# A Perceiver layer on one core: another order of work in the opening, and GpSimd's second K piece and first queries given to ScalarE and VectorE

## What is computed

```python
q = (Q @ Wq + bq) / sqrt(64)   # Q = layernorm(x), 16 heads of 64
k = K @ Wk + bk                # K = V = ctx
v = V @ Wv + bv
x = x + (softmax(q k^T) v) @ Wo + bo           # cross attention
x = x + self_attention(layernorm(x))           # latent K/V, decay, 16 heads of 16
x = x + fp4_ffn(layernorm(x))                  # 256 -> 704 -> 256
```

## Time and profile before

| | us |
|---|---|
| three runs, median | 1313.55 |
| lowest, highest | 1306.68, 1316.39 |
| the profiled execution, its own time | 1306.82 |
| its span in the profile | 1305.0 |

### The profile page before, as it was taken

One profiled execution on the slowest core, in us unless ns is written; L12 is line 12 of the kernel. 1 busy time (PEld: TensorE's weight loads), 2 busy tenths in 40 slices (PEclk: granted clock), 3 DMA queues, 4 the chain that ended last, 5 costly groups with the idle time before them and its releaser, 6 DMA issues.

```text
span 1305.0 us, 25086 instructions
## 1 busy us (share of the span) xinstructions
PE 1267.7 (97%) x9210; PEld 1103.3 (85%) x9210; DVE 879.0 (67%) x1405; ACT 882.2 (68%) x1735; POOL 962.3 (74%) x1132
## 2 busy tenths in 40 slices
PE   5899999999999999999999999999999999999898
PEld 5788888888888888888888888888888888777775
DVE  3566667666766677667766676667666776676657
ACT  3677766777677766777667766777676767676752
POOL 4887898679877986788777987798779868537510
PEclk9999999999999999999999999999999999998999
DMA  4010000000000001101000000000000000300000
GB/s 136 18 29 25 17 1 10 9 18 1 2 18 9 25 18 41 35 23 34 9 10 18 1 2 17 17 2 1 18 1 1 2 9 1 106 2 1 1 1 17
DMA packets 24904, 22.97 MB, mean 18 GB/s; under 512 B 4432, under 2 KB 24528, under 8 KB 24784
## 3 DMA queue, kind: packets, MB, share of 16 engines
q1 hardware_dynamic: 24784, 21.38, 5.5%
HBM read 20.85 MB, written 0.52 MB: 16 GB/s over the span
## 4 chain that ended last, share of the span: by engine, by line
PE 85%; POOL 7%; DVE 3%; ACT 2%; issue 2%; DMA 0%; POOLq 0%; ACTq 0%; DVEq 0%
PE psT L681 17%; PE psS L671 14%; PE psW L709 13%; PE psW L722 12%; PE psO L697 9%; PE psO L698 9%; POOL kT L510 2%; PE saO L931 1%; PE saS L904 1%; PE psW L761 1%; POOL kT L509 1%; PE saO L1035 1%; PE psW L731 1%; POOL v L522 1%; PE psW L744 1%
## 5 line engine op out<-in xcount | busy, mean ns | idle before, releaser
L1217 ACT ACTIVATE pT_hi<-psT 128x512 fp32r<-128x512 f32 x512 | 293.3, 602 | 238.1 <-PE psT L681 235.2
L1453 DVE TENSOR_TENSOR pT_lo<-psT,pT_hi 128x512 fp32r<-128x512 f32 x512 | 330.0, 685 | 103.9 <-ACT pT_hi L1217 102.9
L1447 DVE TENSOR_REDUCE negm<-psS 128x1 f32<-128x1024 f32 x256 | 311.6, 1218 | 20.3 <-PE psS L671 16.8
L510 POOL TENSOR_TENSOR kT<-kraw,khi 64x512 fp32r<-64x512 f32 x252 | 324.1, 1286 | 0.0
L1180 ACT ACTIVATE prob<-psS,negm 128x1024 f32<-128x1024 f32 x256 | 285.8, 1116 | 1.0 <-DVE negm L1447 1.0
L681 PEld LDWEIGHTS psT<-ident,prob 128*128 128x128 f32 x2048 | 230.2, 141 | 62.6 <-issue 36.3
L681 PE MATMUL psT<-ident,prob 128*128 128x128 f32 x2048 | 273.4, 276 | 1.5 <-DVE pT_lo L1453 1.4
L697 PE MATMUL psO<-pT_hi,v 128*128 128x256 f32 x1024 | 268.3, 294 | 0.9 <-POOL v L522 0.9
L698 PE MATMUL psO<-pT_lo,v 128*128 128x256 f32 x1024 | 256.8, 282 | 0.0
L1520 DVE TENSOR_TENSOR oT<-psO,olow 64x256 f32<-64x256 f32 x128 | 53.5, 418 | 214.9 <-ACT olow L1389 214.9
L671 PE MATMUL psS<-kT,q_hi 64*128 64x512 f32 x1024 | 194.5, 416 | 3.4 <-ACT prob L1180 2.0
(11 more groups left out here) (281 smaller groups left out, 1673.8 us busy)
## 6 DMA issues: line engine op xcount, KB each, us to landing
cst<-in_ctx_dram SPq DMA_DIRECT2D x12, 512.0 KB, 3.8
wraw<-in_L_xattn_Wk_dram SPq DMA_DIRECT2D x8, 256.0 KB, 2.6
wraw<-in_L_xattn_Wv_dram SPq DMA_DIRECT2D x8, 256.0 KB, 2.6
wraw<-in_L_xattn_Wq_dram SPq DMA_DIRECT2D x8, 256.0 KB, 2.7
wo<-in_L_xattn_Wo_dram SPq DMA_DIRECT2D x8, 256.0 KB, 2.7
oT<-in_ctx_dram SPq DMA_DIRECT2D x2, 512.0 KB, 5.5
prob<-in_ctx_dram SPq DMA_DIRECT2D x2, 512.0 KB, 4.8
ff_wdn<-in_L_ffn_w_down_dram SPq DMA_DIRECT2D x1, 704.0 KB, 7.4
```

The lines of the kernel that those rows point to most:

```text
L510: pool.tensor_tensor(kT[half, m // 2 % KRING, h, 1, :], raw[own, :], khi[own, :].bitcast(F32), ALU.subtract).then_inc(k_split, 1)
L1217: act.activation(pT_hi[:, i % PRING, :], psT[:, t % 2, :], ACT.Copy).then_inc(ph_ok, 1)
L1447: dve.tensor_reduce(negm[:, g % 2, h, qt, c:c + 1], psS[:, qt, :], AX.X, ALU.max, negate=True)\
L1453: dve.tensor_tensor(pT_lo[:, i % PRING, :], psT[:, t % 2, :], pT_hi[:, i % PRING, :].bitcast(F32), ALU.subtract).then_inc(pl_ok, 1)
```

## The change

It reorders the opening on all five queues and moves two splits off GpSimd.

- SP loads Wk right after x, and Wq into the tile of Wo (`wq_first`), ahead of Wv; Wo's first load waits for Wq's split. Context piece 2 is staged in a tile of the later feed-forward part instead of `prob`.
- TensorE turns context units 0 to 3 before xn, then projects k0, k1, q0, v0, q1, v1, k2, runs scores(0), projects v2, k3, v3 and turns units 4 to 7.
- Piece 1 of K is split from PSUM: three activations on ScalarE (`second_piece_high`), two `scalar_tensor_tensor` on VectorE (`second_piece_low`), which add the bias and subtract the high part. Query pair 0 likewise (`first_pair_high`, `first_pair_low`), three and three. `kraw_ok`, `k_split`, `qraw_ok` and `q_ok` count one less from then on.
- GpSimd splits Wk, Wq, Wv, piece 0, query pair 1, pieces 2 and 3.
- The maxima and exponentials of head 0 come before v2, k3 and v3 on VectorE and ScalarE.

The diff, cut to its changed lines (inner indentation shortened):

```diff
@@ before, line 174 @@
-        staging = [oT[:, i, 0:KPP, :] if i < 2 else prob[:, i - 1, :].rearrange("p (k d) -> p k d", k=KPP)
-                   for i in range(FIRST)]
+        staging = [oT[:, i, 0:KPP, :] for i in range(2)] + [
+  tail.win[:, 0, 0:KPP, :], prob[:, 2, :].rearrange("p (k d) -> p k d", k=KPP)]
@@ before, line 192 @@
+        second_h, second_l, pair0_h, pair0_l = (sem(i) for i in ("second_h", "second_l", "pair0_h", "pair0_l"))
+        wq_first_in = sem("wq_first_in")
@@ before, line 230 @@
+        def pieces_split(m):
+  return 4 * (m if m >= 1 else m + 1)
+        def pairs_split(g, p):
+  return 6 * (2 * g + p)
@@ before, line 238 @@
+        khi_second = pT_hi[:, 0, :]
+        wq_first = wo[:, :, :]
@@ before, line 381 @@
-      wait(sp, wk_ok, 2 * max(g, 1))
-      if g == 1:
-          wait(sp, wq_ok, 2)
+      wait(sp, wk_ok, 2 * g)
@@ before, line 392 @@
+      if g == 0:
+          wait(sp, wq_ok, 2)
@@ before, line 403 @@
+  load_k(0)
...
-  load_k(0)
+  sp.dma_start(wq_first, rows(Wq, 0)).then_inc(wq_first_in, 16)
...
-  load_q(0)
@@ before, line 471 @@
-      wait(pool, raw, 16 * (g + 1))
-      src = wraw[:, slot, :, :]
+      if raw is not raw_q:
+          wait(pool, raw, 16 * (g + 1))
+      elif g:
+          wait(pool, raw_q, 16 * g)
+      else:
+          wait(pool, wq_first_in, 16)
+      src = wraw[:, slot, :, :] if g or w_s is not wq_s else wq_first
@@ before, line 481 @@
-      n = 6 * (2 * g + p)
-      wait(pool, qraw_ok, 2 * g + p + 1)
+      n = pairs_split(g, p) - 6
+      wait(pool, qraw_ok, 2 * g + p)
@@ before, line 499 @@
-      wait(pool, kraw_ok, m + 1)
+      wait(pool, kraw_ok, m if m else 1)
...
-      wait(pool, khi_ok, m + 1)
+      wait(pool, khi_ok, m if m else 1)
...
-      wait(pool, k_split, 4 * m + 4)
+      wait(pool, k_split, pieces_split(m))
@@ before, line 549 @@
+  split_w(0, 1, wq_s, raw_q, wq_ok)
...
-  split_piece(1)
-  split_w(0, 1, wq_s, raw_q, wq_ok)
-  for p in range(2):
-      split_q(0, p)
+  split_q(0, 1)
@@ before, line 660 @@
-          wait(pe, k_split, 4 * (n + 2))
+          wait(pe, k_split, pieces_split(n + 1))
+      if n == 0:
+          wait(pe, second_h, 3)
+          wait(pe, second_l, 2)
+          wait(pe, pair0_h, 3)
+          wait(pe, pair0_l, 3)
...
-          wait(pe, q_ok, 6 * (2 * g + h // 2 + 1))
+          wait(pe, q_ok, pairs_split(g, h // 2))
@@ before, line 763 @@
+  for u in range(4):
+      if u % KT == 0:
+          pe.wait_ge(staged[u // KT], 16)
+      turn_ctx(u, staging[u // KT], bank_S[u])
...
-          last = pe.transpose(bank_S[kt][:, r * P:(r + 1) * P], xn[:, r, kt * P:(kt + 1) * P], ident[:, :])
+          last = pe.transpose(bank_T[kt][:, r * P:(r + 1) * P], xn[:, r, kt * P:(kt + 1) * P], ident[:, :])
...
-  for u in range(4):
+  pe.wait_ge(prep_l, 2)
+  project_k(0, psO[:, :])
+  pe.wait_ge(prep_l, 4)
+  project_k(1, psW[:, :])
+  pe.wait_ge(xnT_l, KT)
+  project_q(0, 0, bank_S[0][:, 0:S])
+  project_v(0, bank_S[2])
+  project_q(0, 1, bank_S[1][:, 0:S])
+  project_v(1, bank_S[3])
+  pe.wait_ge(kraw_ok, 1)
+  project_k(2, psO[:, :])
+  pe.wait_ge(qraw_ok, 1)
+  pe.wait_ge(v_lo, 2)
+  scores(0)
+  project_v(2, bank_T[0])
+  project_k(3, psW[:, :])
+  project_v(3, bank_T[1])
+  for u in range(4, 8):
...
-      turn_ctx(u, staging[u // KT], (bank_S[2], bank_S[3], bank_T[0], bank_T[1])[u])
-  pe.wait_ge(prep_l, 2)
-  project_k(0, psO[:, :])
-  project_v(0, psW[:, :])
-  pe.wait_ge(prep_l, 4)
-  pe.wait_ge(xnT_l, KT)
-  project_k(1, bank_S[0])
-  project_v(1, bank_S[1])
-  pe.wait_ge(staged[2], 16)
-  for u in range(4, 6):
-      turn_ctx(u, staging[2], bank_T[u % 2])
-  project_k(2, bank_S[2])
-  project_v(2, bank_S[3])
-  pe.wait_ge(kraw_ok, 1)
-  project_q(0, 0, psO[:, 0:S])
-  pe.wait_ge(v_lo, 1)
-  project_q(0, 1, psW[:, 0:S])
-  pe.wait_ge(kraw_ok, 2)
-  project_k(3, bank_S[0])
-  pe.wait_ge(v_lo, 2)
-  project_v(3, bank_S[1])
-  pe.wait_ge(staged[3], 16)
-  for u in range(6, 8):
-      pe.wait_ge(prep_l, u - 1)
-      turn_ctx(u, staging[3], bank_T[u % 2])
-  pe.wait_ge(kraw_ok, 4)
-  pe.wait_ge(v_lo, 4)
-  scores(0)
-  pe.wait_ge(prep_l, 8)
+      if u < 6:
+          pe.wait_ge(v_lo, u - 1)
+      else:
+          pe.wait_ge(kraw_ok, u - 4)
+      turn_ctx(u, staging[u // KT], (bank_T[0], bank_T[1], psO[:, :], psW[:, :])[u - 4])
...
-          pe.wait_ge(qraw_ok, 2)
+          pe.wait_ge(prep_l, 8)
@@ before, line 1071 @@
-              wait(pe, qraw_ok, 2 * (g + 1) + (k - 13) // 2 + 1)
+              wait(pe, qraw_ok, 2 * (g + 1) + (k - 13) // 2)
@@ before, line 1087 @@
-          wait(pe, kraw_ok, n + LEAD + 1)
+          wait(pe, kraw_ok, n + LEAD)
@@ before, line 1184 @@
-          wait(act, k_split, 4 * (m - 1))
+          wait(act, k_split, pieces_split(m - 2))
@@ before, line 1197 @@
-      wait(act, q_ok, 6 * (2 * (g - 1) + p + 1))
+      wait(act, q_ok, pairs_split(g - 1, p))
...
+  def second_piece_high():
+      wait(act, k_ps, 2)
+      act.activation(khi_second, psW[:, :], ACT.Identity, bias=bkT[:, 0:1]).then_inc(second_h, 1)
+      for h in range(2):
+          own = slice(HD * h, HD * h + HD)
+          act.activation(kT[HD:2 * HD, 0, h, 0, :], psW[own, :], ACT.Identity, bias=bkT[own, 0:1])\
+              .then_inc(second_h, 1)
+  def first_pair_high():
+      wait(act, q_ps, 1)
+      act.activation(q_hi[:, 0, 0, :], bank_S[0][:, 0:S], ACT.Identity, bias=bqT[:, 0:1]).then_inc(pair0_h, 1)
+      for half in range(2):
+          own, other = slice(HD * half, HD * half + HD), slice(HD - HD * half, 2 * HD - HD * half)
+          act.activation(q_hi[other, 1, 0, :], bank_S[0][own, 0:S], ACT.Identity, bias=bqT[own, 0:1])\
+              .then_inc(pair0_h, 1)
@@ before, line 1317 @@
+  for u in range(4):
+      prep_high(u, bank_S[u])
...
-      act.activation(xnT_hi[:, kt, :], bank_S[kt], ACT.Copy).then_inc(xnT_h, 1)
-  for u in range(4):
-      prep_high(u, (bank_S[2], bank_S[3], bank_T[0], bank_T[1])[u])
+      act.activation(xnT_hi[:, kt, :], bank_T[kt], ACT.Copy).then_inc(xnT_h, 1)
...
-  v_high(0, psW[:, :])
-  k_raw(1, bank_S[0])
-  v_high(1, bank_S[1])
-  for u in range(4, 6):
-      prep_high(u, bank_T[u % 2])
-  k_raw(2, bank_S[2])
-  v_high(2, bank_S[3])
-  for p in range(2):
-      q_raw(0, p, (psO, psW)[p][:, 0:S])
-  v_high(3, bank_S[1])
-  for u in range(6, 8):
-      prep_high(u, bank_T[u % 2])
-  k_raw(3, bank_S[0])
+  second_piece_high()
+  first_pair_high()
+  v_high(0, bank_S[2])
+  q_raw(0, 1, bank_S[1][:, 0:S])
+  v_high(1, bank_S[3])
+  k_raw(2, psO[:, :])
...
+  v_high(2, bank_T[0])
+  k_raw(3, psW[:, :])
+  v_high(3, bank_T[1])
+  for u in range(4, 8):
+      prep_high(u, (bank_T[0], bank_T[1], psO[:, :], psW[:, :])[u - 4])
@@ before, line 1458 @@
+  def second_piece_low():
+      for h in range(2):
+          own = slice(HD * h, HD * h + HD)
+          wait(dve, second_h, 3)
+          dve.scalar_tensor_tensor(kT[HD:2 * HD, 0, h, 1, :], psW[own, :], bkT[own, 0:1],
+                                   khi_second[own, :].bitcast(F32), ALU.add, ALU.subtract).then_inc(second_l, 1)
+  def first_pair_low():
+      wait(dve, pair0_h, 3)
+      dve.scalar_tensor_tensor(q_lo[:, 0, 0, :], bank_S[0][:, 0:S], bqT[:, 0:1], q_hi[:, 0, 0, :].bitcast(F32),
+                               ALU.add, ALU.subtract).then_inc(pair0_l, 1)
+      for half in range(2):
+          own, other = slice(HD * half, HD * half + HD), slice(HD - HD * half, 2 * HD - HD * half)
+          dve.scalar_tensor_tensor(q_lo[other, 1, 0, :], bank_S[0][own, 0:S], bqT[own, 0:1],
+                                   q_hi[own, 0, 0, :].bitcast(F32), ALU.add, ALU.subtract).then_inc(pair0_l, 1)
@@ before, line 1700 @@
+  for u in range(4):
+      prep_low(u, bank_S[u])
...
-      dve.tensor_tensor(xnT_lo[:, kt, :], bank_S[kt], xnT_hi[:, kt, :].bitcast(F32), ALU.subtract)\
+      dve.tensor_tensor(xnT_lo[:, kt, :], bank_T[kt], xnT_hi[:, kt, :].bitcast(F32), ALU.subtract)\
...
-  for u in range(4):
-      prep_low(u, (bank_S[2], bank_S[3], bank_T[0], bank_T[1])[u])
...
-  v_low(0, psW[:, :])
-  v_low(1, bank_S[1])
-  for u in range(4, 6):
-      prep_low(u, bank_T[u % 2])
-  v_low(2, bank_S[3])
-  v_low(3, bank_S[1])
-  for u in range(6, 8):
-      prep_low(u, bank_T[u % 2])
+  dve.wait_ge(bq8_ok, 1)
+  second_piece_low()
+  first_pair_low()
+  v_low(0, bank_S[2])
+  v_low(1, bank_S[3])
...
+  v_low(2, bank_T[0])
+  v_low(3, bank_T[1])
+  for u in range(4, 8):
+      prep_low(u, (bank_T[0], bank_T[1], psO[:, :], psW[:, :])[u - 4])
```

## The result

| | before | after |
|---|---|---|
| median of 17 runs each | 1310.52 us | 1297.65 us |
| lowest, highest | 1306.56, 1319.58 | 1295.35, 1305.89 |
| the profiled execution, own time | 1306.82 | 1300.94 |
| its span | 1305.0 | 1299.0 |

The ratio is 0.9912, with an interval from 0.9895 to 0.9929: faster by 0.88%, which is inside the 1% that the prediction took as the limit of what can be told. The prediction was a ratio of 0.9906 (12.4 of 1313.55 us). Two numbers need care. The medians stand 12.9 us apart, the two profiled executions 5.9, and both differ from the 11.5 that the ratio gives on 1306.8.

A forecast was written before the change was run, and what follows sets the result against it. TensorE's matmul queue bounds the body, which follows the opening. Head 0's turn 11.2 us earlier plus 1.48, together 12.6, less 0.2 for handovers: 12.4 off 1313.55, forecast 1301 us (0.94% less), range 1293 to 1309.

The forecast's parts named there:

- Loads: Opening: context lands at 7.0 and 8.5 us, Wk at 5.6, Wq at 9.3; weight splits finish before use.
- The 0.3 us that the prediction put beside the sum: Norm in the opening: an early Wq would block the last scaling for one GpSimd operation, making the sum 0.3 us larger.
- 24 transposes: TensorE's first work, context then xn, at the lower clock level: 5.13 us, to 12.25; upper level from project_k(0).
- ScalarE and VectorE: Opening splits taken from GpSimd: operations of 0.69 and 0.47 or 0.42 us; v1's low at 21.5, scores(0) at 21.6.
- The scores and what lies under them: Early scores(0), then v2, k3, v3 to 27.5 us; maximum and exponentials run under these, ending at 26.2.
- The drain of 1.38 us: Table load before the first exponential: if added, the exponential starts 0.7 us later and the opening grows about 0.4.
- Head 0: turn(0,0) at 32.4 instead of 43.6 us, 11.2 gained; then 8.66 instead of 10.14 to the next turn, 1.48 more.
- The body: After the opening TensorE is a full queue of matmuls, so whatever the opening gives arrives at the end whole.
- (a): Opening: lower clock level holds on in k0 and k1 and before head 0; gain 8.6, 1305 us; chance 0.14.
- (b): Opening: successive activations overlap and the clock may rise inside the 24 transposes; gain 14.2, 1299 us; chance 0.09.
- (c): After 143.68 us: GpSimd's own backlog turns the gain into a wait; gain 0 to 3, 1312 us; chance 0.08.
- (d): Body: VectorE's later phase delays each head's turn; 0.1 us over 127 heads eats the gain, 0.2 gives 1326; chance 0.05.

The follow-up runs named there:

- experiment 7: The changed kernel with Wk's load moved behind the two context pieces; ratio to before 0.9901, median 1296.43 us.
- experiment 5: The changed kernel with each of VectorE's two subtractions of K piece 1 issued a second time, unread; ratio to before 0.9902, median 1295.95 us.
- experiment 3: The changed kernel with head 0's scores, maxima and exponentials moved back behind v3 and context units 4 to 7; ratio to before 0.9942, median 1302.42 us.
- experiment 6: The changed kernel with two TensorE waits of the opening loosened (scores(0)'s first half, banks of units 5 to 7); ratio to before 0.9883, median 1293.63 us.
- 4: The changed kernel with xn turned ahead of context units 0 to 3; ratio to before 0.9927, median 1298.82 us.
- 8: The changed kernel with GpSimd's addition of the output bias bo moved from step 12 to step 19; ratio to before 0.9863, median 1292.70 us.
- 9: The changed kernel again, unaltered, for a second profile; ratio to before 0.9909, median 1296.99 us.
- 12: The changed kernel with two opening waits loosened, bo added later, and ten idle matmuls in TensorE's self-attention wait; ratio to before 0.9877, median 1290.98 us.
- 1: The kernel before with only the change's loads and order of GpSimd's weight splits; ratio to before 0.9964, median 1303.97 us.
- 11: The changed kernel with both the two loosened opening waits and the later addition of bo; ratio to before 0.988, median 1293.42 us.
- 2: The changed kernel with K piece 1 and query pair 0 split by GpSimd again; ratio to before 0.9966, median 1306.64 us.
- experiment 10: The kernel before with only the addition of bo moved from step 12 to step 19; ratio to before 0.9993, median 1307.76 us.

## Why the prediction was right

The forecast was a gain of 12.4 us; the profile shows 11.80 at the second turn, and the ratio 0.88%, against 0.94. By its steps:

**Loads.** Context was expected at 7.0 and landed at 7.17; TensorE started at 7.31 (7.1). Wk's split was done before the norm's scalings, as expected, and they ended at 9.6 (9.5). The Trainium skill (SBUF — State Buffer, "Who interferes with whom") says that where a VectorE instruction takes the ports it shares with GpSimd, the later of the two blocks fully; this agrees with 404 to 411 ns in after, and 1428 and 1439 ns where GpSimd's subtraction lay beside it (experiment 7). The 0.3 us that the prediction put beside the sum for Wq's split did not come: Wq's split began at 9.56, as the last scaling ended.

**24 transposes.** Taken as 5.13, measured 5.35 (7.31 to 12.66). K piece 0 was at 12.66 (12.25). It took 1.66 us, not 1.39: the upper level came inside it and not before it. That step was wrong by 0.27; piece 1's end came at 15.72 (15.0).

**ScalarE and VectorE.** The new operations were taken too short. I took 0.69 us for the `scalar_tensor_tensor` of 512 columns and 0.42 for 256; they took 0.74 to 0.76 and 0.48 to 0.49, with their distances 0.78 and 0.51. The last low of V was at 22.38 instead of 21.5. From piece 1's end to `scores(0)` it was 6.75 us instead of 6.6. So this term was short by 0.15 only; the other 0.7 of the 0.87 us by which `scores(0)` came late lie ahead of it, in TensorE's start (0.21), the transposes (0.22) and K piece 0 (0.27). VectorE is the right engine (experiment 5).

**The scores and what lies under them.** The second exponential ended at 27.07, not 26.2, under v2, k3 and v3 as expected; v3 ended at 28.59 (27.5). The phrase "3.61 us ... which TensorE sat through before" was too large as a price: undone, the early scores cost 2.3 (experiment 3). The sum did not use the 3.61 and is unharmed. The table load took 1.28 us (22.14 to 23.42), and the exponential started at 24.73, when the maximum was there. The drain of 1.38 us that the Trainium skill adds (ScalarE: Activation LUTs, "What ACT_TABLE_LOAD costs") did not show: in experiment 6 the exponential started 0.18 us behind the load.

**Head 0.** Turned at 33.25 (32.4), 10.4 us earlier instead of 11.2. To the next turn it took 8.73 (8.66 expected, 10.14 before): this saving of 1.4 came whole. Together 11.8 instead of 12.4: 0.85 short at the first turn and 0.07 in head 0, less the 0.2 set off for handovers and the rounding of 12.7 to 12.6.

**The body.** "Whatever the opening gives should arrive at the end whole" held for the 128 heads, but I had looked at it with one stretch of 12 us only the earlier trace rows. Before already had a TensorE wait of 1.88 us at the end of the first group, and whether the clock falls behind it makes 1.58 us. With the tail's 4.3 and the opening's 0.6 this is the 6.5 us by which the profiled execution (1300.94) stands above the 1294.4 forecast for it. Nor is the rest of the body always whole: from the first group's output projection to the last it is 932.4 us in both profiles, but 935.8 to 936.9 in experiments 3 to 6, where the clock was low somewhere between 1148 and 1165 us; this is one reason why the time of a profiled execution says so little about the opening.

**The rivals.** (a) did not come in this form: K piece 1 ran at the upper level (1.40). But its mechanism, a fall of the clock behind a wait, is what took 1.6 us at 162 and most of the 4.3 in the tail of the one profile. (b)'s rise inside the 24 transposes did come in some executions (0.87, 1.01 and 1.11 us for the eight xn transposes in experiments 8, 6 and 9, against 1.71): up to 0.8 us there and 0.3 more in K piece 0; so the phrase of the Trainium skill (TensorE: Matmul & The Clock Gate, Part 1) that the rise varies from run to run agrees with these profiles. (c) fell: GpSimd's chain began 11.76 us earlier, so it moved with TensorE, and the first group's wait is no longer than before. (d) fell: the distance of turns in the body was unchanged, and the lead stayed at 10.27 over 932 us.

The range was said to be 1299 to 1305 widened by half the spread, which is 4.9 us: that gives 1294 to 1310, not 1293 to 1309. Nothing hangs on it.

The forecast time of 1301 was counted from the median of the three runs shown, 1313.55, which lies 3.0 above that of 17. That the measured median came out at 1297.65 is mostly this.

What the falls of the clock cost can be read off the tail, the same code in every profile. Behind the row of the four transposes (the last 2 us of a span left out):

| us at the lower level behind the row | tail, us | profiles |
|---|---|---|
| none | 138.0 to 138.1 | before; 7, 9, 12 |
| 3.4 | 139.3 | 3, 8 |
| 6.8 | 140.9 to 141.0 | 1, 11 |
| 3.4 and 6.8 | 141.0 | 5 |
| 6.8 and 6.8 | 142.4 | after; 2, 10 |
| 17 in two stretches | 143.7, 144.2 | 4, 6 |

In all eight profiles where TensorE waited 4.1 us ahead of that row, the clock fell. In after and experiments 1, 2, 10 and 11 it was low from the four transposes on (1.06 to 1.09 us); in 4, 5 and 6 the transposes still took 0.63 us, and the fall came about 1 us after they had begun (the next score matmuls of that part took 2.05 to 2.06 instead of 1.11). The one profile in which that wait was filled (12) has no fall. What stays open is the shorter waits. The first group's wait of 1.79 to 1.88 us stands in ten profiles, and the clock fell behind it in four (after, 1, 4, 9) and not in six (before, 2, 3, 5, 6, 7). I have no rule for these. That experiment 10 lost its gain in all its executions in the same way is argued from its one profile, not shown.

## What to carry to other kernels

Where the body is full of TensorE work, count only to the first steady turn, and count there by the chain: here the loads alone gave 7.6 of 11.8 us, while taking back one of the other parts cost 7.5 (GpSimd's splits), 2.3 to 3.0 (the early scores) and 1.9 (context first), which adds up to more than the whole, since each takes one place of the same chain. Before blaming a change for a time that does not fit, compare mean granted clocks and take one stretch that the change does not touch (here the tail, 138.0 or 142.4 us with the same code): a second profile of the same kernel was worth more than any edit. And look for waits of 2 to 4 us of TensorE on an engine that is merely ordered badly; moving one addition of 2.4 us took 3.6 us off the changed kernel's first group (4.9 less the 1.3 of a shorter opening) and 4.3 to 5.0 off its median. On the kernel before, the same move also took the wait away and 3.6 us off the first group, but no gain is shown in its median, so look at the later waits too.

## What the runs showed of the hardware that was not expected

- The granted clock fell behind single TensorE waits of 1.80 us (after, 161 us), and the work behind that took 1.58 us longer; behind 1.88 us at the same place in before it did not. It fell behind four of ten such waits of 1.79 to 1.88 us, and by about 1 us after the end of all eight of 4.1 us. Steps of 4 to 5 us between executions of one kernel (1295.4 to 1297.7, then 1300.7 to 1302.5) go with a mean clock of 0.995 and 0.992.
- A low stretch of 6.8 us behind such a wait made the tail 2.9 us longer (140.9 to 141.0 against 138.0); one of 3.4 us ahead of it cost the tail nothing (138.0), since it only shortened the wait to 2.45 us.
- Idle matmuls over 4.48 us, in place of a 4.1 us wait, were followed by 1.00 throughout, where the stretch had 0.66 without them, and cost TensorE 0.02 us.
- Activations of three parts out of one PSUM bank followed one another at 0.71 us for 0.69 us each (15.74, 16.45, 17.16): no overlap, so the handover of 0.02 to 0.03 us is all that lies between them.
